# Narrow attention tiles scaled by ScalarE, one step later, in place of GpSimd

## What is computed

```python
q = _l2norm(q) * scale * qn_g
k = _l2norm(k) * scale * kn_g
scores = jnp.einsum('bhqd,bhkd->bhqk', q, k) * dh ** (-0.5)
scores = jnp.where(causal, scores, jnp.finfo(scores.dtype).min)
attn = jax.nn.softmax(scores, axis=-1)
o = jnp.einsum('bhqk,bhkd->bhqd', attn, v)
```

## Time and profile before

| | |
|---|---|
| median of three executions | 1593.36 us (1590.02 to 1597.71) |
| the profiled execution | 1593.47 us |
| its span | 1591.7 us |
| TensorE busy | 1450.2 us (91%) |
| VectorE busy | 1004.5 us (63%) |
| ScalarE busy | 722.5 us (45%) |
| GpSimd busy | 646.1 us (41%) |
| causal loop, first scores to last weighing | 339.4 to 562 us |
| TensorE, VectorE, ScalarE, GpSimd busy in it | 179.3, 167.3, 128.9, 121.8 us |

### The profile page before, as it was taken

The page is one execution under the profiler, slowest core; times in us unless marked ns, Lnnn a source line. Parts: engine busy times, 40 slices in busy tenths (PEclk is TensorE's granted clock), DMA queues, the critical chain, the costliest instruction groups (busy, mean ns, idle before and its releaser), DMA issues. The chain is left out here.

```text
span 1591.7 us, 22280 instructions
## 1 busy us (share of the span) xinstructions
PE 1450.2 (91%) x8144; PEld 898.6 (56%) x8144; DVE 1004.5 (63%) x1879; ACT 722.5 (45%) x1406; POOL 646.1 (41%) x533
## 2 busy tenths in 40 slices
PE   4888999988888899999999899979999988998998
PEld 2554545446666654454545554546686776776664
DVE  7997254347777702123213321768999999999994
ACT  4442114335656511111111230155788787788783
POOL 4787100045656300000000043016876775776763
PEclk9999999999999999989999999989999999999999
DMA  7001000073122060000000110003011101101001
GB/s 246 2 1 83 0 1 1 0 197 69 35 57 45 1 241 0 0 0 1 0 0 0 42 38 0 1 11 83 1 36 33 34 9 27 33 2 34 1 1 65
DMA packets 28604, 57.03 MB, mean 36 GB/s; under 512 B 7936, under 2 KB 12676, under 8 KB 28240
## 3 DMA queue, kind: packets, MB, share of 16 engines
q1 hardware_dynamic: 27184, 53.03, 12.1%
q10 hardware_dynamic: 1312, 2.56, 0.4%
HBM read 28.77 MB, written 5.84 MB: 22 GB/s over the span
## 5 line engine op out<-in xcount | busy, mean ns | idle before, releaser
L1479 POOL TENSOR_TENSOR tl_ex<-tl_ex,tl_left 128x1250 f32<-128x1250 f32 x80 | 209.8, 2623 | 30.4 <-ACT tl_left L1814 25.7
L1298 DVE SCALAR_TENSOR_TENSOR X<-ex_ps_x,g,X 128x512 f32<-128x512 f32 x80 | 59.9, 750 | 194.3 <-PE ex_ps_x L1191 194.3
L1983 POOL TENSOR_TENSOR lo<-xn,hi 128x512 f16<-128x512 f32 x5 | 5.9, 1188 | 377.3 <-ACT hi L2087 377.3
L1619 PE MATMUL tl_banks<-identf,tl_ex 128*128 128x128 f32 x800 | 134.2, 282 | 24.1 <-ACT tl_pt L1835 14.3
L1835 ACT COPY tl_pt<-tl_banks 128x512 f32<-128x512 f32 (+1 forms) x200 | 108.3, 541 | 91.7 <-PE tl_banks L1619 91.1
L1191 PE MATMUL ex_ps_x<-w,hid 128*128 128x512 f32 (+1 forms) x320 | 144.8, 605 | 0.0
L1164 PE MATMUL ex_ps_h<-yt,w 128*128 128x512 f32 (+1 forms) x384 | 143.3, 527 | 0.0
L1244 ACT ACTIVATE hid<-ex_ps_h,b 128x512 f32<-128x512 f32 (+1 forms) x48 | 29.1, 608 | 245.0 <-PE ex_ps_h L1164 245.0
L1619 PEld LDWEIGHTS tl_banks<-identf,tl_ex 128*128 128x128 f32 x800 | 88.9, 141 | 86.2 <-issue 45.0
L1905 DVE MAX8 tl_m<-tl_banks 128x8 f32<-128x1250 f32 x80 | 116.3, 1454 | 10.0 <-PE tl_banks L1589 9.9
L1911 DVE MAX8 tl_m<-tl_left 128x8 f32<-128x1250 f32 x80 | 117.1, 1464 | 2.8
(11 more groups left out here) (281 smaller groups left out, 2996.8 us busy)
## 6 DMA issues: line engine op xcount, KB each, us to landing
kl<-KT SPq DMA_DIRECT2D x16, 320.0 KB, 4.4
qs<-QO SPq DMA_DIRECT2D x16, 320.0 KB, 6.1
tl_kl<-tl_KT SPq DMA_DIRECT2D x16, 320.0 KB, 4.4
tl_qs<-tl_QO SPq DMA_DIRECT2D x16, 320.0 KB, 6.0
w<-in_L_ffn_W SPq DMA_DIRECT2D x8, 512.0 KB
w<-in_L_ffn_W SPq DMA_DIRECT2D x4, 1024.0 KB, 8.6
at_kept<-AT SPq DMA_DIRECT2D x1, 3200.0 KB, 9.0
AT<-at_kept SPq DMA_DIRECT2D x1, 3200.0 KB, 18.3
```

The lines of the kernel that those rows point to most:

```text
L1479: pool.tensor_tensor(ex[:, n % EXS, 0:N], ex[:, n % EXS, 0:N], left[:, n % LEFT, :], ALU.subtract).then_inc(s_probs, 1)
L1619: mm = pe.transpose(ps_t[:, b * P:(b + 1) * P], ex[:, n % EXS, a + b * P:a + (b + 1) * P], m.identf[:, :])
```

## The change

GpSimd no longer scales the narrow tiles; its queue holds only the splits, one behind the other. ScalarE scales them: normalise(n-2) stands in its step n, for odd n, behind exponentials(n-1) and ahead of keep(n-3, 1). It is an activation (Copy) with the reciprocal as a scale for each partition, in place in ex_small. TensorE waits for the new semaphore probs_a. Nothing else is moved, and the arithmetic is the same.

```diff
--- before.py
+++ after.py
@@ -539,11 +539,11 @@
         s = Stage(nc, m, ctx, "ca")
         (s_rows, s_turned_x, s_cols, s_gained, s_q_ps, s_k_ps, s_v_ps, s_sq, s_summed, s_root, s_inv, s_qn,
          s_qk_turned, s_qk_kept, s_v_kept, s_fetched_0, s_fetched_1, s_staged, s_staged_k, s_scored, s_masked,
-         s_maxed, s_exp, s_inverse, s_probs_d, s_probs_p, s_turned, s_kept_a, s_kept_d, s_weighed, s_o_a,
+         s_maxed, s_exp, s_inverse, s_probs_d, s_probs_a, s_turned, s_kept_a, s_kept_d, s_weighed, s_o_a,
          s_o_d, s_spilled, s_gathered, s_sum_v, s_sum_a, s_near, s_biased, s_owned, s_sums, s_deg, s_added, s_seen,
          s_aggr, s_dev, s_step) = s.signals(
             "rows turned_x cols gained q_ps k_ps v_ps sq summed root inv qn qk_turned qk_kept v_kept fetched_0 "
-            "fetched_1 staged staged_k scored masked maxed exp inverse probs_d probs_p turned kept_a kept_d weighed o_a o_d "
+            "fetched_1 staged staged_k scored masked maxed exp inverse probs_d probs_a turned kept_a kept_d weighed o_a o_d "
             "spilled gathered sum_v sum_a near biased owned sums deg added seen aggr dev step")
         s_fetched = (s_fetched_0, s_fetched_1)
         agg = space("agg0", 86016, [P, KD, NP])
@@ -650,18 +650,9 @@
                 op.then_inc(s_staged, 1)
                 pool.wait_ge(s_staged, 5 * h + step - 1)
 
-            def normalise(n):
-                w = width(SEQ[n % NT])
-                pool.wait_ge(s_inverse, n + 1)
-                pool.tensor_scalar(exps(n)[:, 0:w], exps(n)[:, 0:w], inv[:, n:n + 1], None, ALU.mult
-                                   ).then_inc(s_probs_p, 1)
-                pool.wait_ge(s_probs_p, n // 2 + 1)
-
             for step in (2, 3, 4):
                 stage(0, step)
             for n in range(TN):
-                if n % 2:
-                    normalise(n)
                 h, idx = n // NT + 1, n % NT
                 if h < H and 1 <= idx < 6:
                     stage(h, idx - 1)
@@ -767,7 +758,7 @@
                     return
                 a, w = groups[n][g]
                 if g == 0:
-                    pe.wait_ge(s_probs_p if n % 2 else s_probs_d, n // 2 + 1)
+                    pe.wait_ge(s_probs_a if n % 2 else s_probs_d, n // 2 + 1)
                 q = before[n] + g
                 if q < 2:
                     pe.wait_ge(s_qk_kept, 2 * NT)
@@ -887,6 +878,12 @@
                 act.activation(exps(n)[:, 0:w], logits(n)[:, 0:w], ACT.Exp, bias=negm[:, n:n + 1],
                                accum_out=rsum[:, n:n + 1]).then_inc(s_exp, 1)
 
+            def normalise(n):
+                w = width(SEQ[n % NT])
+                act.wait_ge(s_inverse, n + 1)
+                act.activation(exps(n)[:, 0:w], exps(n)[:, 0:w], ACT.Copy, scale=inv[:, n:n + 1]
+                               ).then_inc(s_probs_a, 1)
+
             def keep(n, g):
                 if not 0 <= n < TN or g >= len(groups[n]):
                     return
@@ -908,6 +905,8 @@
                 keep(n - LAG, 0)
                 if 0 <= n - 1 < TN:
                     exponentials(n - 1)
+                if n % 2 and 0 <= n - 2 < TN:
+                    normalise(n - 2)
                 keep(n - LAG, 1)
                 if n - LAG - 1 in pair_of:
                     keep_o(pair_of[n - LAG - 1])
```

## The result

The changed kernel takes 1597.58 us in the median (1593.94 to 1600.58), against 1593.65 us for the kernel before in the same comparison (16 executions of each): 1.0022 of the time before, 95% interval 1.0013 to 1.0030. The ratio stands for 3.5 us more, the two medians are 3.9 us apart. The forecast was +3.0 us, 1596.5. The profiled execution of after took 1593.94 us, its span is 1592.2.

What follows compares the result with a forecast made beforehand. It took ScalarE's in-order queue, with wide exponentials ahead of the scalings, to replace GpSimd's waits (29.5 to 41.0 us). 1593.5 + 3.0 (six heads +1.4, last head +1.4, last tile 9 some 0.2) = 1596.5 us; range 1589 to 1606.

Steps and rivals of the forecast that it cites:

- The place in ScalarE's queue: Each narrow tile's scaling waits behind the next wide tile's exponential; tile 9 comes 1.20 us late, tile 3 0.84.
- the walk: One causal-loop head followed through tiles 0 to 9 (odd ones narrow), giving each narrow tile's new time; chance 75%.
- The prices: One ScalarE scaling of 128 to 640 columns takes 0.38 to 0.82 us, 3.0 us a head.
- The head: One head of the causal loop grows from 27.25 to 27.48 us.
- The sum: Six heads +1.4 us, first head 0, last head +1.4 and some 0.2 at the last tile 9: +3.0 us.
- The splits in a block: GpSimd's splits run together, 10.3 us, freeing VectorE's scaling of tile 6: 0.69 us instead of 1.32.
- The margin of 0.8 us: Time between VectorE starting to scale tile 2 (458.9) and GpSimd's second subtraction (459.7).
- rival 2: GpSimd's second subtraction holds VectorE's scaling of tile 2, about 2.5 us in six heads: 1611, half hit 1604; chance 14%.
- The copies: ScalarE's copies behind a scaling come 0.4 to 0.8 us later, covered because the weighings come at least as much later.
- Rival 1: GpSimd's waits go and nothing replaces them, 29.5 to 41 us won: 1552 to 1564; chance 4%, a part another 7%.

Runs made afterwards that it cites:

- paced experiment: The changed kernel with each GpSimd split made to wait for ScalarE's scaling of the same tile, undoing the packing alone; 1610.33 us, one execution.
- subtractions last: The changed kernel with GpSimd's five splits reordered, three casts first, then the two subtractions; 1614.29 us, one execution.
- early scaling: The changed kernel with VectorE's narrow reciprocals before the next maximum and ScalarE's scaling before the next wide exponential; 1581.45 us, 0.9909 of before.
- scaling first: The changed kernel with ScalarE's scaling of tile m ahead of the exponential of tile m+1; 1590.68 us, 0.9995 of before.
- kernel that scales twice: The changed kernel with a second activation (Copy, factor 1) and a wait ahead of each of the 40 scalings; 1641.24 us, one execution.

## Why the prediction held

**The place in ScalarE's queue** was right at all five narrow tiles, so the number did not come out by luck. Counted from the start of tile 8's transposes, the walk gives 3.36, 8.56, 13.25, 19.60 and 23.86 us for tiles 9, 1, 3, 5, 7. The head of after that is shown above, the longest of the loop, has 3.35, 8.52, 13.43, 19.78, 24.04. A head like the five others, from 394.86 to 422.39, has 3.34, 8.51, 13.30, 19.65, 23.92 and the next at 27.53: within 0.06 us of the walk everywhere.

**The prices** of the scalings were taken as 0.82, 0.38, 0.49, 0.60, 0.71 us and measure 0.83, 0.39, 0.49, 0.61, 0.71. Taking the nearest row (the activation with a scale out of PSUM) and the slope of the exponential over its columns was enough. The copy out of SBUF costs no more than 0.02 us over the one out of PSUM (0.71 against 0.69 at 512).

**The head** came to 27.55 us, forecast 27.48. The difference has one place: up to tile 1 the usual head (394.86) is 0.05 us ahead of the walk, from tile 3 on 0.05 behind it. Between them lies VectorE's scaling of tile 2. The prediction let it wait for a cast "as much as before". It took 1.20 us in before and takes 1.29 or more in after, and this 0.1 us was left out. That scaling was taken at 1.3 us, since it meets GpSimd's second cast. These are the two rows in a usual head, VectorE and GpSimd:

```profile
403.26 1.29 DVE L1031 TENSOR_SCALAR ex_big<-ex_big,inv 128x1152 f32<-128x1152 f32 x1
402.69 1.25 POOL L644 CAST qh<-qs 64x1280 fp32r<-64x1280 f32 x1
```

In the six heads it takes 1.29 to 1.32 us, but for the 1.42 of the head shown above, whose 27.66 us are 0.11 over the others by it. The cast comes 0.13 us later against the tiles there (7.96 us after tile 8's transposes, 7.83 in the usual head). The cast that I put at 457.7 to 459.0 in that head's time ran from 457.90 to 459.15. The ends written for the first three splits (455.3, 458.3, 459.6) are 4.79, 7.79 and 9.09 us after tile 8's transposes, and the usual head has 4.78, 7.76 and 9.08. But they do not follow from the prices written beside them: a cast of 1.25 from 453.6 ends at 454.85, and a subtraction of 3.3 behind it at 458.15. In the trace the cast, held by VectorE's scaling of tile 0, takes 1.61 us and the subtraction 2.90. That these two were allowed for is not said in the prediction.

**The sum.** Six heads were to give +1.4: the seven intervals give 1.97 together, nearly all of it in six of them, and the first gave nothing, as taken. The last head with what follows was to give +1.6 and gave 1.54 (562.74 - 533.40 = 29.34 before, 564.76 - 533.88 = 30.88 after). Together 3.5 for 3.0.

**The splits in a block** did what was said: tile 6's scaling 0.69 us, and the paced experiment prices it at 0.6 us a head. Without that the change would have been some 4 us slower still. The margin of 0.8 us to rival 2 measured 0.88 in the head shown (second subtraction at 459.23, the scaling asks at 458.35) and 0.76 to 0.79 in the five others.

**The copies** that come later behind a scaling cost nothing, as taken: TensorE's weighings wait for one of ScalarE's copies once, 0.9 us, in before and in after alike.

**Rival 1** fell for the reason given: 42.9 us of ScalarE's waits came where GpSimd's had been. But the forecast of 30 to 40 us for them was not worked out. The walk had it in hand: the five waits of the head above are 1.25 + 0.37 + 1.89 + 0.69 + 1.17 = 5.37, eight times that is 43.0.

**Rival 2** was rightly kept as the slower side, and its 1611 us were near what a block that does hit comes to, 1614.29. But the way there was only half right: the wait gave 28.89 - 27.55 = 1.34 us a head for the 2.5 written, and the falling clock, which the reasoning had left out, gave the rest.

**What was missing**, TensorE's clock, had no effect on this change in the two profiled executions: in before and in after all eight long weighings take 2.40 us, though waits of 2.12 and 1.89 us stand ahead of them. That the forecast needed no term for it was luck: some kernels above with waits no longer than these pay up to 1.67 us in a head. Why the same 1.89 us at tile 3 is followed by a slow weighing in the kernel with the subtractions last is open. TensorE also stands still for 1.32 us at tile 2 there, but in the paced kernel it does not.

## What to carry over

Moving a short operation to an engine with room is priced by what stands ahead of it in that engine's queue. Walk one period with the long operations in their places, and the sum came out here to a tenth of a microsecond a head. Before choosing the engine, ask when the operand is ready and whether the queues let it be used then: bringing the reciprocal and the scaling ahead of the long reduction and exponential (with the splits in another order where GpSimd scales) won about 15 us on either engine (14.6 and 15.5 between the medians), where the change of engine alone won nothing. A new wait on TensorE ahead of a long run of matmuls can cost more than the wait: look at the granted clock of the run behind it.

## What the runs showed of the hardware

**Short waits and TensorE's clock.** The weighing of 38 matmuls takes 2.40 us at a granted clock of 1.00 and up to 4.07 at 0.51 (the 2.4 and 1.2 GHz levels), 1.67 us more. It came in the middle of a busy loop, after short waits, and did not come, in 14 heads of two kernels, where identity matmuls stood in the gap (in the same seven heads of each kernel without them it came four times). It is not the same in every head: with rows alike to 0.01 us ahead of it, a wait of 1.84 us was followed by 4.07 in one head and by 2.40 in another (paced splits), and a wait of 1.26 likewise (early scaling). What separates them no row here shows. TensorE stood still for 1.26 to 2.29 us at tile 3 ahead of the weighings at the lower clock that are shown, and the 2.12 us of before and 1.89 of after at the same place were not followed by one in the executions profiled.

**VectorE and GpSimd.** The length of a VectorE scaling that meets a GpSimd instruction follows from one formula in all kernels here: it ends 0.2 us before GpSimd's record does, plus its own length alone. Four examples: after 459.77 (measured 459.77), subtractions last 409.55 (409.54), scaling first 399.09 + 1.25 - 0.2 + 0.87 = 401.01 (401.00), paced 420.69 + 1.25 - 0.2 + 0.69 = 422.43 (422.42). The longest wait is in the kernel that scales twice: tile 0's scaling takes 3.56 us from 475.76, 2.69 over its own 0.87, beside a subtraction that starts at 475.75. In the paced kernel the scaling's record begins 0.03 us before the cast's, and it waits all the same. The Trainium skill, SBUF — State Buffer, section Who interferes with whom, has it that the wait is for the whole of the other's instruction, and the 2.64 us row agrees. It also has that the one that comes second is held, whichever it is. Here GpSimd is held too: its first cast took 1.64 us for 1.25 where it began at 401.66, during a scaling of VectorE that ran from 401.31 to 402.18 (subtractions last).
